# A fused attention and mixture-of-experts kernel: a regrouped start, spread side operations, and TensorE taking value matmuls before score matmuls in each step

## The chip, the cores and the metric

The kernel runs on one core of one Trainium2 chip. The metric is device microseconds (us) of one execution. The core has five engines with queues of their own: TensorE (PE, matmuls; PEld is its weight load), VectorE (DVE), ScalarE (ACT), GpSimd (POOL) and SyncE (SP), which here only issues DMAs. Engines run in parallel and meet at semaphores; each engine takes its own instructions in program order, so an instruction that waits holds up all that stand behind it.

## The reference

The input is x, 2048 rows of 128 (f32). Three sublayers follow each other:

```python
# causal attention, 16 heads of width 8, with rotary positions
Q = rope((x @ wq.T) by heads); K = rope((x @ wk.T) by heads); V = (x @ wv.T) by heads
scores = where(causal, Q K^T / sqrt(8), -inf)
x = layernorm(x + (softmax(scores) @ V) @ wo.T)
# inner block: attention without a mask, then 8 experts with top-1 routing
y = x + softmax(Q2 K2^T / sqrt(8)) V2 @ w_proj      # Q2, K2, V2 from layernorm(x) @ w_qkv
y = y + expert[argmax(h @ gate_w + gate_b)](h)       # h = layernorm(y); 128 -> 512 -> gelu -> 128
x = layernorm(x + y)
```

So there are two attentions over 2048 positions: number 1 is causal, number 2 is full.

## The kernel before

**Tiling.** The 2048 queries are cut into 4 blocks (`NB`) of 512 (`BLK`), and the keys into tiles of 128. The 16 heads go in 4 groups (`G`) of 4. One *step* is one key tile, one query block and one group: 4 heads x 128 keys x 512 queries. A step has two halves p = 0 and 1 of two heads each. In block qb a group has T steps: 16 in attention 2, 4(qb+1) in attention 1, where the tiles past the diagonal are left out. So attention 1 has 160 steps and attention 2 has 256. The last four steps of each causal group lie on the diagonal: there the query range shrinks (512, 384, 256, 128 queries), and POOL clears the upper triangle (`cut`, line 925, `affine_select` in line 930).

**One half-step.** `scores` (571): two matmuls of 33 rows (32 rows hold the parts of the heads' q and k, row 33 the negative row shift against a row of ones) into a pair of PSUM banks; three pairs rotate, so the scores of half h wait for the exponentials of half h-3. `exps` (823): one ACT instruction reads 128x1024 scores and writes probabilities. It waits for the scores of its half and for the values of half h-4. `values` (581): four columns of the array take 9 columns of V each and add into PSUM bank 6; they wait for the exponentials of the same half, and on the diagonal for POOL's clearing of it. At a group's end DVE copies bank 6 out (`evac`, 1187), PE transposes it (`turn`, 605, three steps into the next group) and DVE divides by the sums (`norm`, 1192).

**The order in a step** is written out in PE's `group` (690 to 719). In step kt PE first issues both halves of the scores of step kt, then the second half of the values of step kt-2 and the first half of those of step kt-1. After that come the turn and the *side operations* of this step: a table `side` says at which step of the block which one stands. DVE follows the same step numbers through `due(step)`.

**Side operations.** In attention 1 (`side1`, 769), while block qb runs, the block before is finished: `post_turn` (5), `post_project` (7), `z_turn` (14), both projections of keys and queries in one call (`project2`, 16), the values (18), key and query norms (20), and `lows` in steps 21 to 24. `lows` samples scores for a lower bound of each row's maximum: in each of these steps two bf16 matmuls into the one PSUM bank 7, each reduced by DVE (`tensor_reduce`, line 1273) before the next may write. Block 3 has no later block to hide behind: its side work stands between the attentions, its `lows` on four banks. In attention 2 the side work is routing and experts.

**Row shifts.** `settle` (534 and 1137) turns norms into the shift of block 0's rows; `final` and `shift_row` (328), or `first_shift_row` (846) on ACT's DMA queue for block 0, write it into `query_rows`. The shifts of blocks 1 to 3 are worked out in block 0's shadow. `general` is a slow exact fallback behind a flag; here the flag is not set, and it costs a flag read and a copy to `negf`. It also times the shift row of the next block: in the last group of a block.

**The start.** For each block PE projects (`project1`), DVE rotates (`split1`, 1054), POOL adds and splits k (`split_k`, 914) between clearing memory with memsets (984), ACT rounds and squares (`first_parts`, 853). SP sends the parts to DRAM (`to_scratch`, 303) and reads them back in row layout (`key_rows`, 308, four DMAs; `query_rows`, 316, eight). SP takes the blocks in order: parts 0, key rows 0, query rows 0, parts 1, key rows 1, parts 2, key rows 2, parts 3, key rows 3, query rows 1, and then two DMAs that fill two rows of `key_rows` with ones (355). Each read-back waits until its parts have landed. Attention 1 waits for the ones (`ld_pad`), block 0's rows, its shift row and all four value projections.

Of the kernel before, what the change touches and what calls it, by code (L numbers as in the profile page):

```python
# [21 lines left out]
ALU = mybir.AluOpType  # L22
# [10 lines left out]
H = 16  # L33
# [37 lines left out]
SHIFT_AT = (None, 4, 6, 8, 9)  # L71
# [18 lines left out]
OPS = len(IN_SHADE)  # L90

# [5 lines left out]
def build(nc, xT_d, x_d, wa_d, wo_d, wqkv_d, wproj_d, ln1w_d, ln1b_d, ln2w_d, ln2b_d, gw_d, gb_d,  # L97
          w1_d, w2_d, cos_d, sin_d, ident_d, blk_d, cmask_d, iota_d, kc_d, out_d):
    ctx = ExitStack()
    with ctx:  # L100
# [121 lines left out]
        ld_a, ld_w, ld_x, ld_e, ld_pad = (sem(n) for n in ("ld_a", "ld_w", "ld_x", "ld_e", "ld_pad"))  # L222
        ld_b = [sem(f"ld_b{b}") for b in range(NB)]
        ld_m, ld_k, z_clear = sem("ld_m"), sem("ld_k"), sem("z_clear")
        init, ones_set, rows_clear = sem("init"), sem("ones_set"), sem("rows_clear")
# [31 lines left out]

        def low_bank(b, i, c):

            return ps[:, 7 if b < NB - 1 else (2 * i + c) % 4, :]  # L260
# [23 lines left out]
        def _(sp):  # L284
# [56 lines left out]
            for b in range(NB):  # L341
# [3 lines left out]
                to_scratch(1, k3, k_scratch, b)  # L345
                sp.wait_ge(A[1]["parts_out"][b % 2], 32 * (b // 2 + 1))
# [3 lines left out]
                if b == 0:  # L350
                    query_rows(1, b)
# [30 lines left out]
            slot_free(2, 1)  # L382
            query_rows(2, 1)
# [36 lines left out]
        def _(pe):  # L420
# [30 lines left out]
            def project2(b):  # L451
# [3 lines left out]
                mm(ps7, wqkv[:, D:2 * D], hT[:, :]).then_inc(s["k_proj"], 1)  # L455
                if b < NB - 1:
                    pe.wait_ge(s["k_taken"], b + 1)
# [25 lines left out]
            def key_bound(a):  # L483

                s = A[a]
                pe.wait_ge(s["kdiag"], 1)
                mm(ps[:, 7, 0:H], onesf[0:H, :], kdg[:, :]).then_inc(s["kmb_mm"], 1)
# [15 lines left out]
            def lows(b, i):  # L503

                t = b * TB + i
                if t == 0:
                    pe.wait_ge(kbd, 1)
                pe.wait_ge(A[2]["nq_taken"], b + 1)
                turn_taken(1)
                for c in range(H * NSUB // BLK):  # L510
                    n = 2 * t + c
                    pe.wait_ge(low_taken, n if b < NB - 1 else max(2 * (NB - 1) * TB, n - 3))
# [982 lines left out]
```

## Time and profile before

| | us |
|---|---|
| median of 3 runs (lowest, highest) | 1136.85 (1129.67, 1142.27) |
| the profiled execution | 1127.68 |
| its span | 1125.9 |
| PE busy | 900.4 (80%) |
| ACT busy | 782.9 (70%) |
| DVE busy | 362.0 (32%) |
| POOL busy | 239.9 (21%) |

The span is what the profiler saw from the first to the last instruction; 1.8 us lie around it. Busy times of PE count matmuls that overlap in the array as one. The granted TensorE clock of the whole span is 0.888 of full speed.

### The profile page before, as it was taken

How to read it: one execution, taken by the hardware profiler on the slowest of the kernel's cores; microseconds unless marked ns; L12 is line 12 of the kernel's file. 1: busy time of each engine (PE TensorE's matmuls, PEld its weight loads, DVE VectorE, ACT ScalarE, POOL GpSimd, SP SyncE). 2: the span in 40 equal slices, each digit the busy share in tenths (PEclk: the TensorE clock that was granted, in tenths of full speed). 3: DMA queues.
4: the chain of work that ended last, by engine and by line, in shares of the span. 5: the costliest groups of instructions: out<-in, count | busy, mean ns of one | idle time of the engine just before them, and what ended most of it. 6: DMA issues, size and time to landing. Idle time of an engine off the chain costs nothing.

```text
span 1125.9 us, 24400 instructions
## 1 busy us (share of the span) xinstructions
PE 900.4 (80%) x9813; PEld 400.4 (36%) x9820; DVE 362.0 (32%) x1027; ACT 782.9 (70%) x906; POOL 239.9 (21%) x360
## 2 busy tenths in 40 slices
PE   5401898897998799439999999999999999996262
PEld 2200443343444334214333444444344444443131
DVE  4440225244014200550000323324433254333563
ACT  1201675785996789119999998898988989884140
POOL 6700411111111101100000032321433212332233
PEclk9655979898998989659999999999999999997565
DMA  7685021111000711273000200012100000000101
GB/s 240 111 160 60 3 40 38 19 23 39 2 2 1 111 22 30 47 161 89 1 2 2 39 25 2 2 28 37 34 2 3 25 11 25 2 2 25 33 1 33
DMA packets 30546, 43.17 MB, mean 38 GB/s; under 512 B 3936, under 2 KB 14944, under 8 KB 30432
## 3 DMA queue, kind: packets, MB, share of 16 engines
q1 hardware_dynamic: 28832, 37.85, 16.8%
q0 software_dynamic: 1536, 3.67, 1.1%
q8 instruction: 79, 1.29, 0.5%
q14 instruction: 35, 0.29, 0.1%
q10 hardware_dynamic: 64, 0.07, 0.0%
HBM read 28.73 MB, written 12.45 MB: 37 GB/s over the span
## 4 chain that ended last, share of the span: by engine, by line
PE 66%; DVE 11%; DMA 9%; ACT 5%; issue 4%; SPq 2%; POOL 1%; another core or an unknown queue 1%; POOLq 0%; ACTq 0%; DVEq 0%
PE ps L422 61%; DMA k_scratch<-parts 4%; ACT probs L829 4%; PE ps L427 3%; DMA key_rows<-ones_f 2%; DVE row_low L1273 1%; PE ps L675 1%; DMA y_sorted<-early_late 1%; DMA query_rows<-neg_shift_final 1%; SPq L322 1%; ACT squares_blockdiag L843 1%; DMA z_rows<-y_sorted,row_shift 1%; POOL z_rows L970 1%; SPq L314 1%
## 5 line engine op out<-in xcount | busy, mean ns | idle before, releaser
L829 ACT ACTIVATE probs<-ps 128x1024 f32<-128x1024 f32 (+3 forms) x832 | 742.8, 1011 | 195.2 <-PE ps L422 193.1
L422 PE MATMUL ps<-probs,values 128*9 128x256 f32 (+1 forms) x6528 | 436.9, 381 | 6.5 <-DVE q_rotated L1190 6.2
L422 PE MATMUL ps<-query_rows,key_rows 33*128 33x512 f32 (+3 forms) x1664 | 337.0, 465 | 73.1 <-DMA key_rows<-ones_f 42.6
L422 PEld LDWEIGHTS ps<-query_rows,key_rows 33*128 33x128 f32 x1664 | 143.0, 190 | 266.8 <-ACT probs L829 119.1
L422 PEld LDWEIGHTS ps<-probs,values 128*9 128x9 f32 x6528 | 145.1, 91 | 220.1 <-issue 120.8
L930 POOL TENSOR_SCALAR_AFFINE_SELECT probs<-probs 128x256 f32<-128x256 f32 x128 | 52.3, 409 | 344.4 <-ACT probs L829 342.0
L1190 DVE COPY q_rotated<-ps 128x512 f32<-128x512 f32 x32 | 22.1, 690 | 217.5 <-PE ps L422 217.4
L963 POOL COPY expert_stage<-early_late 128x512 f32 x72 | 45.4, 668 | 162.1 <-PE ps L422 162.1
L944 POOL DMA_INDIRECT z_sorted<-z_rows,row_shift x16 | 15.8, 990 | 237.3 <-issue 177.0
L959 POOL COPY expert_stage<-parts 128x512 f32 x72 | 47.9, 707 | 44.6 <-PE ps L422 39.1
L900 ACT ACTIVATE expert_stage<-parts 128x512 f32 x24 | 15.1, 630 | 48.7 <-DVE row_shift L1322 27.6
L1197 DVE RECIPROCAL recip<-ps 128x16 f32<-128x16 f32 x32 | 8.2, 257 | 98.0 <-PE ps L427 98.0
L1354 DVE COPY k_work<-ps 128x512 f32<-128x512 f32 x24 | 16.6, 690 | 62.9 <-PE ps L675 62.9
L422 PE MATMUL ps<-expert_stage,k_work 128*32 128x128 f32 x576 | 29.3, 301 | 4.1 <-issue 2.4
L1273 DVE TENSOR_REDUCE row_low<-ps 128x8 f32<-128x512 f32 x32 | 22.1, 692 | 22.2 <-PE ps L422 13.5
L422 PEld LDWEIGHTS ps<-expert_stage,k_work 128*32 128x32 f32 x576 | 24.2, 122 | 13.6 <-issue 6.2
L422 PE MATMUL ps<-early_late,w_attn 128*128 128x512 f32 x32 | 19.9, 780 | 11.4 <-DMA early_late<-in_sin 7.3
L422 PE MATMUL ps<-early_late,k_work 128*32 128x128 f32 x192 | 29.0, 301 | 0.0
L984 POOL MEMSET key_rows<- 32x4096 f32 x8 | 28.0, 3504 | 0.9 <-POOL row_ok L974 0.5
L1129 DVE TENSOR_SCALAR neg_shift<-ps 16x512 bf16<-16x512 f32 x8 | 5.4, 676 | 68.1 <-PE ps L427 68.1
L427 PE MATMUL ps<-ident,z_rows 128*128 128x128 f32 x32 | 6.2, 326 | 22.5 <-DVE z_rows L1051 12.6
L422 PE MATMUL ps<-expert_stage,h_cols 128*32 128x512 f32 x128 | 20.2, 709 | 4.4 <-ACT expert_stage L900 3.3
(166 smaller groups left out, 612.9 us busy)
## 6 DMA issues: line engine op xcount, KB each, us to landing
query_rows<-q_scratch SPq DMA_DIRECT2D x64, 128.0 KB
key_rows<-k_scratch SPq DMA_DIRECT2D x20, 256.0 KB, 7.2
q_scratch<-parts SPq DMA_DIRECT2D x8, 512.0 KB, 3.7
k_scratch<-parts SPq DMA_DIRECT2D x8, 512.0 KB, 4.0
key_rows<-k_scratch SPq DMA_DIRECT2D x16, 192.0 KB, 6.4
parts<-in_w SPq DMA_DIRECT2D x1, 2048.0 KB, 8.3
early_late<-in_w SPq DMA_DIRECT2D x8, 256.0 KB, 7.3
early_late<-z_sorted SPq DMA_DIRECT2D x4, 384.0 KB, 3.1
```

Source lines behind the costliest of these rows:

```text
L422: return nc.tensor.matmul(out, l, r, start=start, stop=stop, skip_group_check=True)
L427: last = nc.tensor.transpose(out[0:m, i * P:(i + 1) * P], rows(i), ident[:, :])
L829: nc.scalar.activation(Pr[:, i % 2, 2 * p:2 * p + 2, lo:BLK], score_banks(t, p)[:, :, lo:BLK], ACT.Exp, scale=SCALE).then_inc(s["exp"], 1)
L900: nc.scalar.activation(w1s[g], W1[:, bass.ds(e * HID, HID)], ACT.Copy).then_inc(m_w1, 1)
L930: nc.gpsimd.affine_select(out=at, in_=at, compare_op=ALU.is_ge, fill=0.0, base=0, pattern=[[0, 2], [1, P]], channel_multiplier=-1).then_in ...
L944: nc.gpsimd.indirect_dma_start(out=z_sorted, out_offset=bass.IndirectOffsetOnAxis(ap=dest[:, i:i + 1], axis=0), in_=zb[:, i, :], in_offset ...
L959: nc.gpsimd.tensor_copy(w1s[g], W1[:, bass.ds(e * HID, HID)]).then_inc(m_w1, 1)
L963: nc.gpsimd.tensor_copy(w2s[g], W2[:, bass.ds(e * HID, HID)]).then_inc(m_w2, 1)
L984: link(nc.gpsimd.memset(KA[at:at + ROWS, part].bitcast(F32), 0.0))
L1190: copy(accs[:, :], sums).then_inc(s["evac"], 1)
L1273: mark(nc.vector.tensor_reduce(low[:, t, hs], low_bank(b, i, c).rearrange("p (h t) -> p h t", t=NSUB), AX.X, ALU.max), low_taken, 2 * t + ...
L1354: mark(copy(hTs2[:, :], side), m_taken, n)
```

## The change

- **Start.** Block 0 is settled alone (norms, bound, shift, flag) after two projections; blocks 1 to 3 follow. The sum and the split of q move from DVE to POOL (`split1` on POOL, `rotate1` and `norms1` on DVE). The memsets between blocks and the ones DMAs go; all 32 pad rows become 1.0, by two ACT copies, one DVE memset and one POOL memset of 32x8192 elements each at the very start. SP's order becomes: parts 0, key rows 0, query rows 0, parts 1, shift row 0, parts 2, key rows 1, query rows 1, parts 3, key rows 2, key rows 3. The key bound is spread a second time for blocks 1 to 3 (`key_bound(1, 2)` at step 0).
- **Side operations.** `project2` is cut in two, each of the eight `lows` matmuls of a block gets a step of its own, and the steps stand in a table `SIDE1_AT` for each block.
- **Block 3's `lows`** move from between the attentions into steps 4 to 11 of attention 2's block 0; its shift turns move to steps 17 to 25. `query_rows(2, 1)` is issued after the first shift row has landed.
- **`general`** of the causal block 0 runs one group earlier.
- **Order in a step.** PE takes the values first and the scores second.

```diff
-SHIFT_AT = (None, 4, 6, 8, 9)
+SHIFT_AT = {1: (None, 5, 6, 8, 9), 2: (None, 17, 21, 23, 25)}
+LOWS_AT = tuple(range(4, 12))
+SIDE1_AT = {
+    1: (13, 14, 15, 17, 20, 21, (22, 23, 24, 25, 26, 28, 29, 30)),
+    2: (13, 17, 19, 21, 23, 25, (28, 30, 32, 34, 36, 38, 40, 42)),
+    3: (14, 17, 20, 22, 24, 26, (28, 30, 32, 34, 36, 38, 40, 42)),
+}
...
+def general_group(causal, qb):
+    return G - 2 if causal and qb == 0 else G - 1
...
+            parts_sent(0)
+            first_key_rows(0)
+            query_rows(1, 0)
+            parts_sent(1)
+            shift_row(1, 0)
+            parts_sent(2)
+            first_key_rows(1)
             query_rows(1, 1)
-            sp.wait_ge(rows_clear, 1)
-            for at in (ROWS, HALF + ROWS):
-                sp.dma_start(kaf[at:at + 1, :, :].rearrange("o h (c t) -> o (h c) t", t=P),
-                             onesf[0:1, :].unsqueeze(1).to_broadcast([1, PAIRS * S // P, P])).then_inc(ld_pad, 16)
+            parts_sent(3)
+            first_key_rows(2)
+            first_key_rows(3)
...
-            slot_free(2, 1)
-            query_rows(2, 1)
             sp.wait_ge(A[2]["parts_out"][1], 64)
...
-            sp.wait_ge(low_mm, 2 * S // P)
             sp.wait_ge(A[2]["c_row"], 32)
+            slot_free(2, 1)
+            query_rows(2, 1)
...
                 for kt in range(T):
-                    for p in range(2):
-                        scores(s, qb % 2, g, kt * P, t0 + kt, mine[kt]["lo"], p)
                     if kt == 0 and before is not None:
                         values(a, before[-2], 1)
                         values(a, before[-1], 0)
...
                     if kt >= 2:
                         values(a, mine[kt - 2], 1)
                         values(a, mine[kt - 1], 0)
+                    for p in range(2):
+                        scores(s, qb % 2, g, kt * P, t0 + kt, mine[kt]["lo"], p)
...
+            project1(0)
+            project1(1)
+            key_norms(1, 0)
+            query_norms(1, 0)
             settle(1)
+            general(1, 0, 0)
+            for b in range(1, NB):
+                if b + 1 < NB:
+                    project1(b + 1)
+                key_norms(1, b)
+                query_norms(1, b)
             attention(1, side1, after1)
...
-            for i in range(TB):
-                lows(b, i)
             settle(2)
...
+            act.wait_ge(ones_set, 1)
+            for at in (ROWS, HALF + ROWS):
+                nc.scalar.activation(KAv[at:at + ROWS, :, S // 2:S],
+                                     onesf[at:at + ROWS, 0:1].unsqueeze(2).to_broadcast([ROWS, PAIRS, S // 2]),
+                                     ACT.Copy).then_inc(rows_set, 1)
...
+            link(nc.gpsimd.memset(KAv[ROWS:2 * ROWS, :, 0:S // 2].bitcast(F32), 1.0))
...
+            nc.vector.memset(KAv[HALF + ROWS:P, :, 0:S // 2].bitcast(F32), 1.0).then_inc(rows_set, 1)
...
+            rotate1(0)
+            norms1(0)
+            rotate1(1)
             settle(1)
+            general(1, 0)
```

## Rows read from the trace of the kernel before

**Rows 1.** The page's chain of waits: shares of the span by engine.
```profile
PE 66%; DVE 11%; DMA 9%; ACT 5%; issue 4%; SPq 2%; POOL 1%; another core or an unknown queue 1%; POOLq 0%; ACTq 0%; DVEq 0%
```

**Rows 2.** Windows by stage: length, busy PE, PEld, DVE, ACT, POOL, clock, DMA, GB/s.
```profile
0.00:107.60 107.60, 30.03 (x110) 14.96 (x110) 37.27 (x88) 11.96 (x21) 40.47 (x22) 0.67 0.74 149
107.60:142.40 34.80, 28.27 (x302) 14.17 (x302) 6.41 (x17) 20.90 (x32) 13.00 (x32) 0.84 0.02 5
142.40:456.80 314.40, 282.62 (x2972) 122.38 (x2976) 86.69 (x253) 242.97 (x288) 39.31 (x96) 0.93 0.18 31
456.80:499.80 43.00, 12.08 (x44) 6.59 (x46) 29.35 (x101) 2.56 (x5) 3.10 (x2) 0.62 0.39 75
499.80:1026.30 526.50, 511.89 (x6084) 221.71 (x6088) 151.55 (x415) 486.13 (x530) 112.36 (x169) 0.99 0.09 22
```

**Rows 3.** Chain of waits in the start: start us, us, what.
```profile
33.80 19.58 DMA k_scratch<-parts
...
88.54 19.01 DMA key_rows<-ones_f
```

**Rows 4.** Timeline of the start: start us, us, engine, line, operation, [idle before <-releaser].
```profile
3.47 7.07 POOL L984 MEMSET key_rows<- 32x4096 f32 x2 [0.47 <-POOL row_ok L974]
...
53.45 0.63 ACT L861 ACTIVATE parts<-k_work 128x512 fp32r<-128x512 f32 x1 [10.95 <-DMA k_scratch<-parts]
```

**Rows 5.** Timeline at the first scores of attention 1's block 1.
```profile
141.59 1.22 PE L422 MATMUL ps<-query_rows,key_rows 33*128 33x512 f32 x4 [4.86 <-DMA query_rows<-neg_shift_final]
```

**Rows 6.** Timeline of PE in one step of attention 2 without side work.
```profile
603.65 0.91 PE L422 MATMUL ps<-query_rows,key_rows 33*128 33x512 f32 x4
...
604.49 1.05 PE L422 MATMUL ps<-probs,values 128*9 128x256 f32 x16
605.47 0.19 PEld L422 LDWEIGHTS ps<-query_rows,key_rows 33*128 33x128 f32 x2 [0.43 <-issue]
```

**Rows 7.** Timeline of ACT over the same stretch.
```profile
602.95 11.14 ACT L829 ACTIVATE probs<-ps 128x1024 f32<-128x1024 f32 x12
```

**Rows 8.** Timeline where ACT waits for scores, and PE then for ACT.
```profile
129.91 0.73 PE L422 MATMUL ps<-query_rows,key_rows 33*128 33x512 f32 x4
...
130.50 1.02 ACT L829 ACTIVATE probs<-ps 128x1024 f32<-128x1024 f32 x1 [0.90 <-PE ps L422]
...
500.71 2.86 ACT L829 ACTIVATE probs<-ps 128x1024 f32<-128x1024 f32 x3 [24.24 <-PE ps L422]
501.78 0.29 PEld L422 LDWEIGHTS ps<-query_rows,key_rows 33*128 33x128 f32 x2 [1.04 <-ACT probs L829]
```

**Rows 9.** Timeline of one diagonal step: exponentials, then POOL's clearing.
```profile
123.73 3.35 ACT L829 ACTIVATE probs<-ps 128x1024 f32<-128x1024 f32 x4 [0.91 <-PE ps L422]
...
125.00 0.41 POOL L930 TENSOR_SCALAR_AFFINE_SELECT probs<-probs 128x256 f32<-128x256 f32 x1 [1.62 <-ACT probs L829]
```

**Rows 10.** Groups by form: exponentials over 256 queries; busy, mean ns.
```profile
L829 ACT ACTIVATE probs<-ps 128x512 f32<-128x512 f32 x32 | 18.9, 641 | 5.8 <-PE ps L422 5.7
```

**Rows 11.** Windows: a causal group, a full group, a full group with experts.
```profile
298.10:318.80 20.70, 20.18 (x238) 8.71 (x236) 1.72 (x5) 19.84 (x24) 3.19 (x9) 1.00 0.01 3
...
561.60:591.30 29.70, 29.35 (x328) 11.68 (x326) 1.30 (x4) 29.44 (x33) 0.00 (x0) 1.00 0.01 2
684.80:720.40 35.60, 34.87 (x462) 15.67 (x464) 12.32 (x22) 31.52 (x37) 13.69 (x23) 1.00 0.01 2
```

**Rows 12.** Timeline of PE: scores of two neighbouring steps that hold sampled scores.
```profile
373.37 0.73 PE L422 MATMUL ps<-query_rows,key_rows 33*128 33x512 f32 x4
...
376.58 0.73 PE L422 MATMUL ps<-query_rows,key_rows 33*128 33x512 f32 x4
```

**Rows 13.** Timeline between the attentions.
```profile
477.07 5.77 DVE L1273 TENSOR_REDUCE row_low<-ps 128x8 f32<-128x512 f32 x8 [0.55 <-remote]
...
490.71 1.32 ACTq L851 DMA_DIRECT2D query_rows<-neg_shift_final  x2
...
499.82 1.65 PE L422 MATMUL ps<-query_rows,key_rows 33*128 33x512 f32 x6 [10.67 <-DMA query_rows<-neg_shift_final]
```

More of the change, by code:

```diff
@@ L339, in slot_free, with parts_sent @@
                     sp.wait_ge(A[1]["S"], 2 * first_step(True, NB - 1 + b))
-            for b in range(NB):
+            def parts_sent(b):
                 sp.wait_ge(A[1]["q_split"], b + 1)
@@ L501, in query_norms, with lows @@
                 last.then_inc(s["nq_mm"], 1)
-            def lows(b, i):
-                t = b * TB + i
-                if t == 0:
+            def lows(b, n):
+                i, c = n // 2, n % 2
+                if b == n == 0:
                     pe.wait_ge(kbd, 1)
                 pe.wait_ge(A[2]["nq_taken"], b + 1)
[L509 to L512, printed above, removed]
-                    mm(low_bank(b, i, c), sq[:, 2, i * P:(i + 1) * P], kblk[:, c * BLK:(c + 1) * BLK]).then_inc(low_mm, 1)
+                turn_taken(1 if b < NB - 1 else 2)
+                if b == NB - 1:
+                    pe.wait_ge(A[2]["flag"], 1)
+                pe.wait_ge(low_taken, 2 * b * TB + n)
+                mm(ps7, sq[:, 2, i * P:(i + 1) * P], kblk[:, c * BLK:(c + 1) * BLK]).then_inc(low_mm, 1)
             def shift_turn(a, b):
@@ L712, in group @@
                         values(a, mine[kt - 1], 0)
+                    for p in range(2):
+                        scores(s, qb % 2, g, kt * P, t0 + kt, mine[kt]["lo"], p)
                     if kt == TURN_STEP and n:
                         turn(a, n - 1, after.get(g))
[L715 removed]
+                        if g == general_group(causal, qb) and qb + 1 < NB:
                             general(a, qb + 1, t0 + TURN_STEP + 1)
@@ L726, in attention @@
                     pe.wait_ge(s["q_taken"], NB)
-                general(a, 0, 0)
+                if not causal:
+                    general(2, 0, 0)
                 mine = None
@@ L763, in side0 @@
             def side0(a):
-                todo = {SHIFT_AT[b]: [lambda b=b: shift_turn(a, b)] for b in range(1, NB)}
-                todo[SHIFT_AT[NB]] = [lambda: count_ok(a, 2)]
+                at = SHIFT_AT[a]
+                todo = {at[b]: [lambda b=b: shift_turn(a, b)] for b in range(1, NB)}
+                todo[at[NB]] = [lambda: count_ok(a, 2)]
+                if a == 1:
+                    todo[0] = [lambda: key_bound(1, 2)]
+                else:
+                    for n, p in enumerate(LOWS_AT):
+                        todo[p] = [lambda n=n: lows(NB - 1, n)]
                 return todo
@@ L806, in _ @@
             query_norms(2, b)
-            for i in range(TB):
-                lows(b, i)
             settle(2)
@@ L1237, in split2 @@
                 if b < NB - 1:
+                    due(at[2])
                     dve.wait_ge(s["q_proj"], b + 1)
@@ L1252, in split2 @@
                     mark(tt(sq[:, 0, :], qa[:, :], qa[:, :], ALU.mult), s["sq_q"], b + 1)
-                    due(18)
+                    due(at[3])
                     dve.wait_ge(s["v_proj"], b + 1)
@@ L1369, in attention @@
                 causal = a == 1
-                general(a, 0)
                 if causal:
@@ L1373, in attention @@
                 else:
+                    general(2, 0)
                     link(ts(before[:, :], cmask[:, :], 0.0, None, ALU.is_lt))
@@ L1383, in attention @@
                     if qb + 1 < NB:
-                        events.append(((G - 1) * T + TURN_STEP, lambda: general(a, qb + 1)))
+                        events.append((general_group(causal, qb) * T + TURN_STEP, lambda: general(a, qb + 1)))
                     events.sort(key=lambda e: e[0])
@@ L1408, in attention @@
                     else:
+                        if causal:
+                            spread_key_norms(1, 2)
+                        else:
+                            take_lows(NB - 1, LOWS_AT, due)
                         shift(a, 1, NB)
                         for b in range(1, NB):
-                            due(SHIFT_AT[b])
+                            due(SHIFT_AT[a][b])
                             take_shift(a, b)
-                        due(SHIFT_AT[NB])
+                        due(SHIFT_AT[a][NB])
                         take_ok(a, 2)
```

126 lines of the change are left out of this document (63 added, 63 removed).

## The prediction

> **What bounds it now.** I read the chain of waits first: 66% of the span hangs on PE, 5% on ACT [rows 1]. Such a share mixes stages, so the windows by stage come next [rows 2]. Five stretches matter. In the start, 107.6 us, PE is busy for 30 and the DMA engines for 0.74 of the time; the chain there is two long transfers, 19.6 us for the parts of block 1 and 19.0 us until the ones have landed [rows 3]. Block 0 of attention 1 takes 34.8 us, its blocks 1 to 3 take 314.4, the gap between the attentions 43.0, attention 2 takes 526.5. After that a tail follows that the change does not touch.
>
> What bounds a step is read from the timeline, and it decides this case. A step of attention 2 without side work takes 1.82 us on PE: 0.84 for both score halves, 0.98 for both value halves [rows 6]. ACT does 12 exponentials in 11.14 us without a break [rows 7]; less the last one's own 1.02, that is 0.92 per half, 1.84 per step. So both run at one pace, and ACT is never without work, because PE issues the scores of step kt before it waits for the exponentials that its values need.
>
> **The order in a step.** Before: S(2k), S(2k+1), V(2k-3), V(2k-2), where S, V and E of a number are scores, values and exponentials of that half. After: V(2k-3), V(2k-2), S(2k), S(2k+1). V(2k-2) waits for E(2k-2), and now S(2k) stands behind it in PE's queue, and E(2k) waits for S(2k). That closes a loop from E(2k-2) to E(2k), once per step. Its pieces:
> - an exponential that found no backlog took 1.02 us [rows 8];
> - PE went on 0.05 after its end: start 500.71 plus 1.02 is 501.73, the weight load began at 501.78 [rows 8];
> - a value half is half of 0.98, 0.49 [rows 6]; I take 0.55, as the change of operands to the scores lies behind this half alone;
> - from the first score matmul to the start of the exponential 0.59 (129.91 to 130.50) [rows 8].
>
> Sum 2.2 us per step against 1.83: plus 0.37. The bounds are 2.1 (value half 0.49, start of the exponential 0.05 sooner) and 2.3 (if the exponentials stay as long as with backlog for part of the steps). One step of each group escapes: at kt=1 only one value half stands ahead, whose exponential is old, so it stays at 1.83. In a step with side work X, PE has 2.2 minus its own 1.82 to spare before V(2k) is due, so a step costs the larger of 2.2 and what it cost before; it is not the sum.
>
> *Attention 2.* A group without side work took 29.7 [rows 11]; it becomes 15 x 2.2 + 1.83 = 34.8, plus 5.1. Block 0 has four such: plus 20. The `lows` and shift turns put there are a few tenths of PE each, in steps of their own, and fit in the spare 0.38. In blocks 1 to 3 a group with experts took 35.6 [rows 11], 2.2 on average, but mixed from steps of 1.83 and longer ones. By the step tables 25 of a block's 64 steps carry side work; the other 39 go up by 0.37: 14, less about 1 for the four steps after a group's end, where the wait for the copy of the sums is now inside the loop. Three blocks: 39. Together plus 59, less 2 for the same wait in block 0: **plus 57**. With 2.1 or 2.3 in place of 2.2 it is 42 or 73.
>
> *Attention 1, blocks 1 to 3.* Full-width steps behave alike. On the diagonal V(2k-2) waits for POOL too. The first exponential there ended at 123.73 + 1.02 = 124.75, POOL began at 125.00 and took 0.41 [rows 9]; PE's reaction I put at 0.1 (between nothing and POOL's own 0.25). That is 0.76 in place of 0.05, in the loop. Before, the two score halves and V(2k-3) covered it. The exponentials shrink from 1.02 to 0.64 at half width [rows 10], so by 0.19 per tile; value and score parts shrink from 1.14 in all to an estimated 0.7. The four diagonal steps become about 2.9, 2.6, 2.2, 1.7 = 9.4. A quiet group of 12 steps took 20.7 [rows 11]: 8 x 1.83 = 14.6 and 6.1 for the diagonal. It becomes 8 x 2.2 + 9.4 - 0.4 = 26.6. Groups of 8 and 16 steps go from 13.4 to 17.8 and from 28.0 to 35.4. Four groups of each: from 248 to 319.
>
> *Side operations.* The stretch really took 314.4 [rows 2], so 66 lie above its quiet groups: side work, waits and stretches at the lower clock. A step with two sampled scores took 3.21 (373.37 to 376.58) [rows 12], 1.39 more than a quiet one, twelve times: 17. Each now has a step, one matmul, and a reduction of 0.7 on DVE that has the whole step: nothing. Of the other 49, the projections and z turns mostly sink into the spare 0.38 of more steps. I leave 30: two post steps per block, the excess of four large side matmul groups, waits for DVE's chains, and half-clock stretches after the diagonals, where PE will be busy for less than half of 9 us. If nothing of the 49 sinks it is 49, if the low clock stays away 18. 319 + 30 = 349 against 314: **plus 35** (23 to 54).
>
> **The start.** The memsets: POOL cleared 32x8192 elements in 7.07 [rows 4], and POOL and DVE pay that once while the inputs load. ACT's copy of 512 elements took 0.63 [rows 4], so at most 10 us for 8192, with 1.02 for 1024 as the nearer price 8; two end at 16 to 22, when ACT's first rounding is due at about 17: no loss to 5 us. Sum and split of q move to POOL, 1.27 each there, two more per block; POOL has lost 28 us of memsets. Block 0's parts go out about 1 us later. Then SP's queue decides: parts 1 stand behind key rows 0 and query rows 0 as before, landed at 53.4 [rows 3, 4]. Block 3's rounding on ACT waits for them, and v_taken of block 3 gates attention 1. Shift row 0 stands right behind parts 1 and its flag comes at about 35, so it lands by 56. Attention 1 starts at **58** rather than 107.6, 49 sooner.
>
> But block 1 of attention 1 can't follow as soon. SP still has parts 2, key rows 1, query rows 1, parts 3, key rows 2 and 3 to move, and only then shift row 1. That is what filled 53.4 to 107.6 before, less the ones, some 4 us: about 105 with the shift row's own 2. Block 0's 16 steps are all diagonal: 4 x 9.4 = 38, and at the lower clock, in which the start ended (0.67 over the stretch [rows 2]), 2 more per group and 4 for the turns: 50, ending at 108. Both give the first scores of block 1 at **about 107**, against 141.6 with its 4.9 us wait for the shift row [rows 5]: **minus 35**. Bounds: 100 (full clock) and 115 (ACT's copies late, low clock throughout). `general` a group sooner removes that 4.9, which is in this number; what is late next is that same shift row, behind key rows 3.
>
> **The gap.** Eight reductions, 5.8 us, stood alone on DVE [rows 13]. The shift row was issued at 490.7 to 492.0 and scores began at 499.8: 7.8 for two 16 KB transfers, behind the eight query-row transfers of block 1 that SP had just issued. These now follow it; I take 2 to 3 us for it. Minus 5.8 and minus 5: **minus 11** (6 to 12). Query rows 1, W1 and W2 are needed a block later.
>
> **Sum**: 57 + 35 - 35 - 11 = plus 46, on the profiled execution's 1127.7: 1174. That execution lies 9.2 below the median of 1136.85 and below all three runs, so I forecast 1174 + 9 = **1183** as a median.
>
> **Rivals.**
> *The loop is covered (faster).* Should the exponential of S(2k) start without waiting for V(2k-2) to pass, nothing is lost in the order: minus 35, minus 36 (66 to 30 in the side work), minus 11 give 1046, 1055 as a median. It decides at a loop of 1.83, which needs 0.37 of the 1.19 us of latency and matmuls to vanish. For it speaks that matmul ends are modelled; against it that PE issues in program order and each piece has a row. 0.08.
> *Half covered.* The loop is nearer 2.0, the diagonals cost half, and the side work sinks wholly: 1125 to 1150. 0.13.
> *The clock.* PE gets gaps of 0.38 us in each step of attention 2, where the granted clock was 0.99 with PE busy for 512 of 526.5 [rows 2]. At 1.2 GHz PE's own work is 2 x 1.82 = 3.64 per step, so attention 2 would take 930 and the whole about 1500; a fifth of the steps, 1250. Against it: block 0 of attention 1 held 0.84 with PE busy for 28 of 34.8 [rows 2], less than the 83% to come. 0.04. The Trainium skill (TensorE: Matmul & The Clock Gate, "A second HAM failure mode: psum-queue depth-cycling") has a matmul kernel whose frequent micro-idles made the clock swing between its two levels; by that rule this rival would be the likely one, and the rows of attention 2 can't refute it, since they hold no such gaps.
> *The start is not earlier.* If ACT's copies or POOL's longer chain delay parts 1 by 10 us, both ends of the start move: 1193 to 1215. 0.08.
>
> The likeliest has the remaining 0.67, 1150 to 1210. I count 1% (11 us of the median) as no change. Slower: 0.67, 0.12 from clock and start, 0.02 of the half-covered: 0.81. Within: 0.08. Faster: 0.08 and 0.03: 0.11. The range of 8 in 10 reaches from 1128 to 1212.
>
> **What would show it.** ACT's exponentials at 1.02 us each, with a gap before every other one, released by PE scores; starts of score pairs 2.2 apart; a quiet full group of 34.8 and a quiet causal group of 12 steps of 26.6; weight loads of the values waiting for ACT and, on the diagonal, POOL; first scores at 58, block 1's at 107, and a gap of 32. Quiet full groups at 29.7 would make the forecast wrong; so would attention 2 at a clock well under 1.

## The result, and the profile after

The change made the kernel slower: 1179.88 us as the median of 4 runs (1171.62 to 1189.43) against 1137.38 for the kernel before on the same chip (1129.67 to 1142.27, 4 runs), a ratio of 1.0356 with a 95% interval of 1.0264 to 1.0448. Forecast were 1183, in a range of 1128 to 1212. Ratios leave out slow executions, more than 1.5% above the fastest of their kernel, which the medians keep, so that a ratio here can differ a little from the quotient of two medians. The profiled execution has a span of 1184.6 us, 58.7 above that of before.

The windows by stage come first, as before, cut at PE's first scores of each stage (columns as in [rows 2]):

```profile
0.00:55.40 55.40, 26.97 (x110) 13.91 (x110) 34.02 (x60) 26.36 (x23) 30.52 (x23) 0.85 0.80 202
55.40:96.50 41.10, 32.70 (x314) 13.95 (x312) 14.20 (x41) 20.47 (x32) 12.99 (x32) 0.79 0.84 125
96.50:449.90 353.40, 304.69 (x2927) 111.18 (x2939) 83.84 (x248) 246.93 (x286) 38.14 (x94) 0.86 0.13 25
449.90:491.20 41.30, 15.04 (x73) 8.97 (x65) 22.04 (x80) 3.21 (x7) 4.08 (x5) 0.57 0.39 71
491.20:1083.50 592.30, 527.23 (x6037) 192.82 (x6040) 160.19 (x440) 500.40 (x528) 112.85 (x169) 0.99 0.10 21
```

Compare PE's share in the last line: 527 of 592, where it was 512 of 526.5 [rows 2]. PE has a little more to show as busy and 50 us more in which it waits. The stages of all kernels below are cut at the first and the last exponential of each stage, which gives slightly other lengths than [rows 2]:

| us | before | after | difference | forecast |
|---|---|---|---|---|
| start | 108.5 | 56.3 | -52.2 | |
| attention 1, block 0 | 34.0 | 41.2 | +7.2 | -35 with the start |
| attention 1, blocks 1 to 3 | 309.2 | 353.4 | +44.2 | +35 |
| gap | 49.1 | 41.3 | -7.7 | -11 |
| attention 2 | 524.0 | 592.4 | +68.4 | +57 |
| tail | 101.2 | 100.0 | -1.2 | 0 |
| span | 1125.9 | 1184.6 | +58.7 | +46 |

**The loop.** The chain of waits by engine, first line of that part of the page, has changed its owner in part: ACT had 5% of the chain [rows 1] and now has 22.

```profile
PE 55%; ACT 22%; DVE 6%; issue 6%; DMA 6%; POOL 2%; SPq 2%; POOLq 1%; ACTq 1%; DVEq 0%
```

The timeline shows the whole loop in a quiet step of attention 2 (start us, us, engine, line, operation, count, [idle before <-releaser]):

```profile
605.92 1.94 ACT L862 ACTIVATE probs<-ps 128x1024 f32<-128x1024 f32 x2 [0.29 <-PE ps L437]
605.98 0.12 PEld L437 LDWEIGHTS ps<-probs,values 128*9 128x9 f32 x8 [0.37 <-ACT probs L862]
605.98 0.62 PE L437 MATMUL ps<-probs,values 128*9 128x256 f32 x8
607.00 0.12 PEld L437 LDWEIGHTS ps<-probs,values 128*9 128x9 f32 x8 [0.90 <-ACT probs L862]
607.00 0.62 PE L437 MATMUL ps<-probs,values 128*9 128x256 f32 x8 [0.39 <-ACT probs L862]
607.54 0.30 PEld L437 LDWEIGHTS ps<-query_rows,key_rows 33*128 33x128 f32 x4 [0.43 <-issue]
607.55 0.73 PE L437 MATMUL ps<-query_rows,key_rows 33*128 33x512 f32 x4
608.14 1.94 ACT L862 ACTIVATE probs<-ps 128x1024 f32<-128x1024 f32 x2 [0.29 <-PE ps L437]
```

Follow it once round. The first of the pair of exponentials starts at 605.92 and takes 1.02, so it ends at 606.94. PE starts its values at 607.00, 0.06 later. The scores start at 607.55, 0.55 after that. ACT starts on them at 608.14, 0.59 later. 1.02 + 0.06 + 0.55 + 0.59 = 2.22, and 608.14 - 605.92 = 2.22. Every piece stands where the forecast had it. ACT rests 0.29 in each step and PE 0.39; neither engine is full, and each waits for the other.

Windows of whole groups: a quiet full group of attention 2, a causal group of 12 steps in attention 1, and 4 us just after a diagonal:

```profile
566.60:601.90 35.30, 29.88 (x326) 9.18 (x324) 1.30 (x4) 30.94 (x33) 0.00 (x0) 1.00 0.01 2
...
172.60:203.00 30.40, 26.89 (x250) 9.97 (x248) 10.82 (x48) 20.60 (x24) 3.26 (x8) 0.78 0.24 33
...
205.00:209.00 4.00, 4.00 (x32) 1.75 (x32) 0.81 (x1) 1.82 (x2) 0.00 (x0) 0.50 0.01 4
```

The first answers to the 29.70 of [rows 11]. A quiet causal group of 12 steps, forecast at 26.6, doesn't occur: the four groups of block 2 took 30.0 to 34.8. In the second the clock is 0.78, in the third 0.50, which is the lower of its two levels, 1.2 GHz, and PE is busy all the time: the wait on the diagonal is followed by slow matmuls.

**The diagonal** has POOL's clearing in the same loop (timeline, last full-width step of a group):

```profile
367.55 1.94 ACT L862 ACTIVATE probs<-ps 128x1024 f32<-128x1024 f32 x2 [0.29 <-PE ps L437]
...
368.73 0.41 POOL L972 TENSOR_SCALAR_AFFINE_SELECT probs<-probs 128x256 f32<-128x256 f32 x1 [29.73 <-ACT probs L862]
...
369.29 0.62 PE L437 MATMUL ps<-probs,values 128*9 128x256 f32 x8 [0.74 <-POOL probs L972]
...
369.84 0.62 PE L437 MATMUL ps<-query_rows,key_rows 33*128 33x384 f32 x4
370.38 1.51 ACT L862 ACTIVATE probs<-ps 128x768 f32<-128x768 f32 x2 [0.90 <-PE ps L437]
```

367.55 to 370.38 is 2.83 for this step. The three after it take 2.57, 2.08 and 2.03 where nothing else disturbs them, 9.5 in all. In block 2, where the clock is often at the lower level, the four took 10.9 to 13.1.

**The start.** The chain of waits in the start (start us, us, what), and then PE's first scores of block 0 and of block 1:

```profile
33.31 17.36 DMA k_scratch<-parts
...
59.29 22.71 DMA k_scratch<-parts
...
83.88 10.49 DMA key_rows<-k_scratch
```

```profile
55.38 1.22 PE L437 MATMUL ps<-query_rows,key_rows 33*128 33x512 f32 x4
...
96.54 1.22 PE L437 MATMUL ps<-query_rows,key_rows 33*128 33x512 f32 x4
```

**The gap**, timeline of its last part:

```profile
476.71 1.26 POOL L1035 TENSOR_TENSOR parts<-q_work,parts 128x512 f32<-128x512 f32 x1 [24.85 <-ACT q_work L922]
477.09 0.89 DVE L1121 TENSOR_TENSOR k_norm_max<-k_norm_max 16x1 f32<-16x1 f32 x1
...
477.91 1.89 POOL L1038 COPY values<-early_late 128x2048 f32<-128x2048 f32 x1
...
478.27 1.55 DVE L1126 TENSOR_SCALAR k_norm_diag<-ident,k_norm_max 16x16 f32<-16x16 f32 x1
...
487.65 1.90 ACTq L884 DMA_DIRECT2D query_rows<-neg_shift_final  x2
...
491.24 0.80 PE L437 MATMUL ps<-query_rows,key_rows 33*128 33x512 f32 x2 [5.15 <-DMA query_rows<-neg_shift_final]
```

The shift row went out at 487.65, 3.1 earlier than before [rows 13], and scores followed 3.6 later where it had been 9.1. The two DVE operations at 477.09 and 478.27 are odd: on 16 partitions, and 0.89 and 1.55 us long. More on them at the end.

### The profile page after: what moved, and what is told of

It is laid out like the page before. It is cut to its first block, busy times and chain, and to the rows that moved or that the text cites. A ratio compares the mean times of both kernels' runs of the same rounds, so it can differ in the third digit from the quotient of the medians.

```text
span 1184.6 us, 24409 instructions
## 1 busy us (share of the span) xinstructions
PE 943.3 (80%) x9808; PEld 361.8 (31%) x9822; DVE 365.2 (31%) x1022; ACT 817.6 (69%) x908; POOL 230.5 (19%) x361
## 4 chain that ended last, share of the span: by engine, by line
PE 55%; ACT 22%; DVE 6%; issue 6%; DMA 6%; POOL 2%; SPq 2%; POOLq 1%; ACTq 1%; DVEq 0%
PE ps L437 51%; ACT probs L862 20%; DMA k_scratch<-parts 4%; PE ps L442 2%; PE ps L694 1%; ACT key_rows L899 1%; POOL probs L972 1%; DMA key_rows<-k_scratch 1%; SPq L329 1%; SPq L321 1%; POOL z_rows L1012 0%; DMA z_rows<-y_sorted,row_shift 0%; DMA y_sorted<-early_late 0%; DVE ln_stats L1079 0%; DVE squares_blockdiag L1371 0%
## 5 line engine op out<-in xcount | busy, mean ns | idle before, releaser
L862 ACT ACTIVATE probs<-ps 128x1024 f32<-128x1024 f32 (+3 forms) x832 | 763.1, 973 | 235.7 <-PE ps L437 235.5
L437 PE MATMUL ps<-probs,values 128*9 128x256 f32 (+1 forms) x6528 | 501.2, 391 | 118.3 <-ACT probs L862 81.9
L437 PE MATMUL ps<-query_rows,key_rows 33*128 33x512 f32 (+3 forms) x1664 | 318.5, 460 | 6.4 <-DMA query_rows<-neg_shift_final 5.2
L437 PEld LDWEIGHTS ps<-probs,values 128*9 128x9 f32 x6528 | 118.3, 91 | 421.0 <-ACT probs L862 327.4
L437 PEld LDWEIGHTS ps<-query_rows,key_rows 33*128 33x128 f32 x1664 | 135.0, 197 | 192.2 <-issue 158.4
L437 PE MATMUL ps<-expert_stage,k_work 128*32 128x128 f32 x576 | 29.2, 300 | 4.3 <-DVE attn_rows L1237 1.6
L442 PE MATMUL ps<-ident,q_rotated 128*128 128x128 f32 x128 | 21.9, 296 | 1.7 <-DVE q_rotated L1227 1.7
L437 PEld LDWEIGHTS ps<-early_late,k_work 128*32 128x32 f32 x192 | 21.3, 120 | 0.0
```

The lines of the kernel that those rows point to most:

```text
L437: return nc.tensor.matmul(out, l, r, start=start, stop=stop, skip_group_check=True)
L442: last = nc.tensor.transpose(out[0:m, i * P:(i + 1) * P], rows(i), ident[:, :])
L862: nc.scalar.activation(Pr[:, i % 2, 2 * p:2 * p + 2, lo:BLK], score_banks(t, p)[:, :, lo:BLK], ACT.Exp, scale=SCALE).then_inc(s["exp"], 1)
```

## The experiments

All ratios are to the kernel before, with 95% intervals. First the order in a step alone, in both directions; then the parts of the rest.

**1. The change without its new order.** The changed kernel, with the scores first in each step as before.

```diff
                 for kt in range(T):
+                    for p in range(2):
+                        scores(s, qb % 2, g, kt * P, t0 + kt, mine[kt]["lo"], p)
...
                         values(a, mine[kt - 1], 0)
-                    for p in range(2):
-                        scores(s, qb % 2, g, kt * P, t0 + kt, mine[kt]["lo"], p)
```

> The changed kernel with the order in a step put back: both score halves first, then the value halves. If the loop E(2k-2), V(2k-2), S(2k), E(2k) is what the new order costs, a quiet step of attention 2 goes from 2.23 back to 1.83 us, attention 2 from 592 to about 524 to 530 between its first and last exponential, blocks 1 to 3 of attention 1 from 353 to about 280, and the span is about 97 + 280 + 41 + 526 + 100 = 1044. If the steps are long for another reason (the side operations in more steps, or the lower clock), the quiet step stays above 2.0 and the span above 1120.

Measured: 1058.56 us (1054.49 to 1062.89), ratio 0.9246 (0.9172 to 0.9321). So all the rest of the change is worth 7.5%, and the order costs more than all of it. Windows of blocks 1 to 3 of attention 1 and of attention 2:

```profile
96.60:373.80 277.20, 267.34 (x2937) 115.92 (x2939) 84.86 (x248) 241.33 (x286) 38.70 (x93) 0.96 0.17 32
...
412.60:951.20 538.60, 516.35 (x6025) 221.28 (x6025) 158.45 (x440) 486.81 (x528) 112.66 (x169) 0.98 0.11 23
```

353.4 against 277.2 and 592.3 against 538.6: with the start and the gap at about the same length, the order costs 76 and 54 us in these two stages. The clock in the first went from 0.96 to 0.86 with it. Attention 2 lies 9 us above the 530 expected here; the last section follows them up to a hold-up of PE.

**2. The new order alone.** The kernel before with the same few lines moved the other way: values first, nothing else of the change.

```diff
                 for kt in range(T):
-                    for p in range(2):
-                        scores(s, qb % 2, g, kt * P, t0 + kt, mine[kt]["lo"], p)
...
+                    for p in range(2):
+                        scores(s, qb % 2, g, kt * P, t0 + kt, mine[kt]["lo"], p)
```

> The kernel before with only the order in a step changed: values first, scores second. By the loop: quiet steps of 2.23 in place of 1.82, attention 2 about 590 rather than 524, blocks 1 to 3 of attention 1 about 365 rather than 309, block 0 about 42 rather than 34, the start unchanged at 108: a span of about 1250. If the order does its harm only together with the spread side operations, the span stays under 1180.

Measured: 1286.50 us (1283.00 to 1293.88), ratio 1.1221 (1.1138 to 1.1305). A quiet full group in its windows is the same 35.30 as in the changed kernel:

```profile
658.80:694.10 35.30, 29.87 (x326) 9.12 (x324) 1.31 (x4) 30.90 (x32) 0.00 (x0) 1.00 0.01 2
```

The span of 1292 is 42 above the expected 1250: blocks 1 to 3 took 382 where 365 stood, with the clock at 1.2 GHz for 121 us of them, and attention 2 took 604 where 590 stood.

The four kernels make a square. The order multiplies the time by 1.122 on the old rest and by 1.0356 / 0.9246 = 1.120 on the new one; within the intervals these are equal. In microseconds they are less alike, 143 and 121 by the medians. One reason is visible: block 0 takes 9.7 longer with the order on the old rest and no longer on the new one, where in either order it ends with a wait for block 1's shift row.

**3. Scores between the value halves.** The loop says that only V(2k-2), whose exponential is fresh, must not stand ahead of the scores. Here PE takes V(2k-3), S(2k), S(2k+1), V(2k-2) (at kt=2 both value halves behind the scores).

```diff
+                    elif kt >= 3:
+                        values(a, mine[kt - 2], 1)
+                    for p in range(2):
+                        scores(s, qb % 2, g, kt * P, t0 + kt, mine[kt]["lo"], p)
...
-                        values(a, mine[kt - 2], 1)
                         values(a, mine[kt - 1], 0)
-                    for p in range(2):
-                        scores(s, qb % 2, g, kt * P, t0 + kt, mine[kt]["lo"], p)
```

> The changed kernel with a third order: the old value half V(2k-3), then both score halves, then V(2k-2). Only the value half whose exponential is old stands ahead of the scores, so the loop is open. By the loop theory the quiet step is 1.83 and the span within 10 us of that of the scores-first order, 1035 to 1055. If it is putting values ahead of scores as such that costs (switching of operands twice a step, later scores), the quiet step is 1.95 or more and the span 1080 or more.

Measured: 1086.08 us (1084.50 to 1091.45), ratio 0.9477 (0.9408 to 0.9546). The quiet step is 1.81, as with the scores first: it is that one value half which closes the loop, not the place of values as such. But the kernel is 27.5 us slower than the first experiment, where at most 10 were expected. A quiet group takes 30.1 in place of 29.6, and the timeline shows the step with the transposes, two halves of values and a turn between two pairs of scores:

```profile
506.50 0.73 PE L437 MATMUL ps<-query_rows,key_rows 33*128 33x512 f32 x4
...
507.71 0.66 PE L442 MATMUL ps<-ident,q_rotated 128*128 128x128 f32 x4
...
508.85 0.73 PE L437 MATMUL ps<-query_rows,key_rows 33*128 33x512 f32 x4
509.45 2.86 ACT L865 ACTIVATE probs<-ps 128x1024 f32<-128x1024 f32 x3 [0.34 <-PE ps L437]
```

From scores to scores 2.35, and ACT ran dry for 0.34 before it. This step is 2.29 long by its exponentials, and 1.85 with the scores first. So in this step the score pairs come too late behind the old value half and the transposes. That accounts for some 0.45 us in each group of attention 2; the rest of the 27.5 was not traced step by step (blocks 1 to 3 are 19 us longer, with 40 us at 1.2 GHz against 20, and attention 2 is 11 longer).

**4 and 5. No clearing on the diagonal**, in the changed kernel (values first) and in the first experiment (scores first). Both leave out the masking on the diagonal: POOL does nothing there, and the values wait for the exponentials alone.

```diff
-                             cut=2 * (n * TB + kt % TB) + 1 if causal and kt >= qb * TB else None,
+                             cut=None,
...
-                    if causal:
-                        with pool.Fori(0, G) as g:
-                            group(qb, g)
```

> The changed kernel (values first) without POOL's clearing of the upper triangle on the diagonal and without PE's wait for it; the masking is left out, nothing else. If POOL's 0.25 + 0.41 + 0.1 us stand in the loop on the diagonal, the last four steps of a causal group shorten from 9.5 to about 6.7 to 7 us, 64 steps by 0.7 each: a span some 40 to 50 us shorter, 1135 to 1145, a little less still if the clock is lower for less of the time. If the clearing is hidden, as it was before, the span stays at 1175 to 1185.

Measured: 1146.12 us (1140.30 to 1149.49, 10 runs), ratio 1.0000 (0.9964 to 1.0036).

> The changed kernel with scores first and without POOL's clearing of the upper triangle and PE's wait for it; the masking is left out. A control for the run without clearing and values first. If the clearing is covered by the scores and by V(2k-3) in this order, the time stays within 10 us of the scores-first run (1055 of span). If the clearing costs by itself, wherever it stands, the span is some 30 to 40 us shorter here too.

Measured: 1038.58 us (1036.69 to 1047.66), ratio 0.9223 (0.9143 to 0.9304). Windows with values first: two causal groups of 12 steps; then with scores first: blocks 1 to 3 whole.

```profile
219.20:243.50 24.30, 22.22 (x246) 7.58 (x244) 4.29 (x9) 20.59 (x24) 0.00 (x0) 1.00 0.07 26
243.50:267.90 24.40, 22.04 (x242) 7.50 (x240) 4.48 (x9) 20.62 (x25) 0.00 (x0) 1.00 0.01 3
```

```profile
98.50:369.10 270.60, 261.68 (x2946) 115.41 (x2957) 82.82 (x248) 241.59 (x287) 0.00 (x0) 0.98 0.17 32
```

In blocks 1 to 3 the clearing costs 353.4 - 305.7 = 48 us behind the values and 277.2 - 270.6 = 7 us behind the scores. Without it the last four steps of a group take 2.17, 1.90, 1.41 and 1.36, 6.85 in place of 9.5; over 12 groups that is 32. The other 16 I put down to the clock: it was at 1.2 GHz for 95 us of these blocks in the changed kernel and for 10 without the clearing. The blocks fit this on the whole: 4 x 2.65 is 10.6, and with the clearing block 1, with 7 of the 95 us, is 7.6 longer, block 3, with 20, is 10.2 longer, and block 2, with 68, is 29.9 longer. (In the same stage the kernel before had 44, the first experiment 20.)

The kernel with scores first became 19.9 shorter by its span, more than the 10 of a covered clearing and less than the 30 of one that isn't. 7 are the clearing's; 12.6 lie in attention 2, which has nothing to clear (see the last section).

**6. The old side table on the first experiment.** Scores first, all else of the change, but the side operations in the old steps, `lows` two per step.

```diff
-SIDE1_AT = {
-    1: (13, 14, 15, 17, 20, 21, (22, 23, 24, 25, 26, 28, 29, 30)),
...
-}
+SIDE1_AT = {q: (14, 16, 16, 18, 20, 20, (21, 21, 22, 22, 23, 23, 24, 24)) for q in (1, 2, 3)}
...
-                    todo[p] = [lambda n=n: lows(b, n)]
+                    todo.setdefault(p, []).append(lambda n=n: lows(b, n))
```

> The changed kernel with scores first and with the side operations of attention 1 at the step numbers of the kernel before (two sampled scores a step again, keys and queries in one step). If spreading them is worth what the steps of 3.2 us showed, blocks 1 to 3 of attention 1 go from 277 up to about 305, near the 309 of the kernel before, and the span to about 1083. If it is not the spreading but the earlier start or the clock that made that stretch shorter, it stays at 277 to 285.

Measured: 1073.85 us (1071.08 to 1077.59), ratio 0.9518 (0.9445 to 0.9592). Blocks 1 to 3 take this in the windows, with a clock of 0.95 in place of 0.96:

```profile
98.40:401.60 303.20, 274.19 (x2947) 119.21 (x2951) 84.68 (x248) 242.19 (x287) 38.50 (x95) 0.95 0.15 29
```

303.2 against 277.2: spreading is worth 26 us there. The spans differ by 15.5 only: the rest is lost in attention 2, where the two kernels are the same code and yet the first experiment takes 538.7 and this one 528.0; see the last section. The medians lie 15 apart as well, the ratios 0.027, which is 31 us: the two were timed on different chips, and the executions of the kernel before that are in the ratio have a median of 1129.2 here and of 1143.9 there. The size in the whole is between 15 and 31.

**7. The shift row of block 1 before the key rows.** In the first experiment PE finished block 0 at about 85 and then waited; the chain of waits there shows for what:

```profile
84.75 0.69 SPq L339
...
85.48 10.90 DMA query_rows<-neg_shift_final
```

DVE had started on the last copy of the row at 79.3, but SP issued it behind the key rows of blocks 2 and 3, and its two small transfers took 10.9 us among theirs. This edit moves it up:

```diff
             parts_sent(3)
+            shift_row(1, 1)
             first_key_rows(2)
             first_key_rows(3)
```

> The changed kernel with scores first and with shift row 1 issued before key rows 2 and 3. In the profile with scores first, block 0 was done at 85, the shift row was issued at 84.7 and landed at 96.4 behind key rows 3. If that queue place is what block 1 waits for, its first exponential comes at 86 to 88 rather than 97.5 and the span goes from 1055 to about 1045. If block 1's own key and query rows are late as well, it stays at 95 or more.

Measured: 1036.79 us (1031.80 to 1054.41, 7 runs), ratio 0.9170 (0.9112 to 0.9228). It was run again beside a repeat of the first experiment:

> The changed kernel with scores first, once more, beside the next one on the same chip: a span of 1035 to 1058, the spread coming from short stretches at the lower clock in attention 2.

> Scores first and shift row 1 ahead of key rows 2 and 3, once more, beside the run before on the same chip: 10 to 13 us less than it, all of it before the first scores of block 1.

Measured: the first experiment again 1056.62 us (1050.80 to 1058.99), ratio 0.9237 (0.9163 to 0.9312); the early shift row again 1048.88 (1045.70 to 1057.34), ratio 0.9166 (0.9101 to 0.9232). The timelines of SP and PE of this last one:

```profile
81.78 1.35 SPq L339 DMA_DIRECT2D query_rows<-neg_shift_final  x2
83.25 5.11 SPq L321 DMA_DIRECT2D key_rows<-k_scratch  x8
```

```profile
86.83 0.73 PE L439 MATMUL ps<-query_rows,key_rows 33*128 33x512 f32 x4
```

Block 1 starts at 86.8 in place of about 97, and block 0 takes 29.2 where it took 40.1: 11 us, as the chain had promised. By medians 7.8 of them arrive, and the two intervals overlap. In the profiled execution attention 2 was 6 longer, with 38 us at 1.2 GHz against 17 in the repeat of the first experiment. So the gain at its place is shown, its size in the whole is not. By its ratio it is the fastest version of all, 8.3% under the kernel before.

**8. The ones without their DMAs, on the kernel before.** POOL's memsets write 1.0 in place of 0.0, and the two DMAs at the end of SP's start go.

```diff
-            for at in (ROWS, HALF + ROWS):
-                sp.dma_start(kaf[at:at + 1, :, :].rearrange("o h (c t) -> o (h c) t", t=P),
-                             onesf[0:1, :].unsqueeze(1).to_broadcast([1, PAIRS * S // P, P])).then_inc(ld_pad, 16)
...
-                    pe.wait_ge(ld_pad, 32)
+                    pe.wait_ge(rows_clear, 1)
...
-                    link(nc.gpsimd.memset(KA[at:at + ROWS, part].bitcast(F32), 0.0))
+                    link(nc.gpsimd.memset(KA[at:at + ROWS, part].bitcast(F32), 1.0))
```

> The kernel before with the two ones DMAs taken away: POOL's memsets between the blocks write 1.0 rather than 0.0, and attention 1 waits for them in place of the DMAs. The prediction put the ones at some 4 us of the DMA stretch and so block 1's first scores in the changed kernel at 107; they came at 97. If the ones cost about 4, attention 1 starts at 103 to 105 here rather than 107.6. If they were the mis-sized piece, it starts at 96 to 99 and the span is about 10 us shorter. If it starts at 104 or later, what was faster in the changed kernel is the order of its transfers.

Measured: 1116.81 us (1110.92 to 1121.59), ratio 0.9781 (0.9709 to 0.9854). The end of the start in its chain of waits, and the issue of block 0's shift row in its timeline:

```profile
67.32 7.91 DMA key_rows<-k_scratch
75.23 0.11 issue
75.34 1.55 PE ps L419 x6
```

```profile
65.51 1.91 ACTq L848 DMA_DIRECT2D query_rows<-neg_shift_final  x2
```

First scores at 75.3 against 107.6: 32 us from these two transfers alone, where at most 12 were expected. The chain names key rows, but PE needs only those of block 0 here, and they had landed at 35.6; the wait that ended last is the one for block 0's shift row, whose last piece landed at 75.20. In the kernel before it had landed at 76.14, so attention 1 then waited 31 us for the ones alone. Those 31 us are not the ones' own time. Just ahead of them in SP's queue stand block 1's query rows. From their issue to the last landing it took 25.3 us with the ones (82.29 to 107.55) and 22.9 without (81.02 to 103.95). So the ones made the run of transfers only some 2.3 us longer, and cost 32 because they stood at its end. By medians 27.7 arrive; in the profiled execution it is 16.8, as 13.7 are given back in attention 2.

## Why the prediction was right, and where it was off

The direction and the mechanism were right: the order closes a loop from exponential to exponential, and what the rest of the change gains is less than what that costs. Point by point:

**The loop of 2.2 us.** Measured 2.23 per quiet step, from pieces of 1.02, 0.06, 0.55 and 0.59 against 1.02, 0.05, 0.55 and 0.59. The step at kt=1 stayed at 1.83 as said. A quiet full group took 35.3 where 34.8 stood.

**Attention 2, +57, measured +68.4.** (The upper bound, worked out with 2.3, comes to 76 and not 73.) In blocks 1 to 3 it is 44 where 39 stood: the quiet step is 0.42 longer, not 0.37, and 39 steps of three blocks make 6 of that. Block 0 went up by 24.7 where 18 stood. Its first group took 39.2 in place of 31.3: the clock was at 1.2 GHz for the first 14.2 us of attention 2, against 7 before, and there the steps took 3.0 to 3.55. The forecast had no term for that.

**Blocks 1 to 3 of attention 1, +35, measured +44.2.** The diagonal was right at full clock: 9.4 said, 9.5 measured. The mis-sized term is the low clock behind it, priced at about 12 us. It was there for 95 us in place of 44, and the fourth experiment puts 16 us of time on the clock that the clearing brings. The side operations behaved as the first experiment shows: with the scores first, these blocks fell from 309.2 to 277.2, by 32, where the fall from 66 to 30 in this term had said 36. So the two halves of the term were +76 for the order (said: 71) and -32 for the rest (said: -36).

**Start and block 0, -35, measured -45.** First scores at 55.4 where 58 stood; block 1's at 96.5 where 107 stood, outside the bounds of 100 and 115 on the good side. The step that failed is "That is what filled 53.4 to 107.6 before, less the ones": it takes the same transfers to need the same time in a new order. The ones were not what was mis-sized: 4 said, 2.3 by the eighth experiment. But from the landing of parts 1 to the last row of this stretch there were 51.9 us there (52.02 to 103.95) and 43.7 in the changed kernel (50.67 to 94.37), so 8 us went with the order. In the old order block 1's eight query-row transfers stand last; from 92 to 104 us they keep the DMA engines busy for 0.46 of the time in the eighth experiment. In the new order they are issued at 53.3, land at 79.3 and share that time with parts 2 and 3, at a share of 0.86 to 1.11 from 55 to 75 us. No run changed that order alone, so the 8 us are a difference of two traces. The key rows of block 3 landed at 94.4 where 103 stood. That block 0 would take 50 us was wrong too: its steps took 36, near the 38 said for full clock, and with 4 us of waiting for block 1's shift row it came to 41. The two errors had the same sign. The wait for block 1's shift row behind the key rows, named as the next thing late, was real: the seventh experiment takes it away and gains 11 us at that place with the scores first.

**The gap, -11, measured -7.7.** The transfers gave 5.5 where 5 stood. The 5.8 us of reductions gave only 2.2. Behind them stood DVE's own chain of norms and now two of its operations waited for POOL instead.

**The sum.** +58.7 by the profiled executions against +46. That the forecast of 1183 lies 3 from the median of 1180 is partly luck: the profiled execution after (1184.6 of span) was above its median, the one before was below. The terms were off by 10, 9, 3 and 11 us, with one of them on the other side. By the medians the difference is 42.5, so the two ways to measure it lie 16 us apart, more than any of these errors.

**The rivals.** The loop covered was refuted by the trace, and its figure of 1055 is near what the same kernel does with the scores first, 1058.56. That is partly luck: by parts the first experiment shows -45, -32, -10 and, in attention 2, +15, where that sum had -35, -36, -11 and nothing. The loop half covered fell with the 2.23. The start not earlier fell with first scores at 55.4. The clock: from 506.4 to the end of attention 2 this window shows 1.00 (the columns are those of [rows 2]), with PE resting 0.39 in each quiet step.

```profile
506.40:1083.50 577.10, 512.86 (x5945) 187.96 (x5945) 159.50 (x439) 490.81 (x518) 112.85 (x169) 1.00 0.08 19
```

The pattern told in the Trainium skill (TensorE: Matmul & The Clock Gate, "A second HAM failure mode: psum-queue depth-cycling") did not come here in attention 2. What did come is that waits on the diagonals are followed by stretches at 1.2 GHz, 95 us of blocks 1 to 3 against 10 without the clearing.

## What to carry to other kernels

In a queue that is worked in order, put the work that feeds the next engine ahead of the work that waits for that engine's last result; a single half ahead of it turned a step of 1.81 us into one of 2.23, though neither engine was full. Find the price before building by adding the pieces of the loop from rows where that engine had no backlog. And when a transfer or an operation goes, read what the waiting engine needs otherwise: the price of the ones was the distance to the next wait, block 0's shift row 32 us earlier, though they had made the run of transfers only 2.3 us longer.

## What the runs showed of the hardware

**DVE behind POOL.** In the gap an operation on 16x1 elements took 0.89 us and one on 16x16 took 1.55. They ended at 477.98 and 479.82; POOL's add ended at 477.97 and its copy at 479.80. The second of these took 0.22 in the kernel before, where the eight reductions held DVE until POOL was done. The Trainium skill (SBUF — State Buffer, "Summary: rules for kernel authors") says that the one issued second waits until the first is done if DVE works in its mode with two ports, or has two inputs in SBUF while the GpSimd operation reads SBUF. The ends in this trace agree; which of the two the 16x16 operation meets, the trace doesn't tell. In the first experiment POOL's add began 0.10 after the first of these two and not 0.38 before it: the two took 0.15 and 0.66, and the second again ended 0.02 after POOL's add. No run here moved the copy away, so how much of the gap it would give was not measured.

**A hold-up of PE that the profile does not explain.** The first group of experts in attention 2 is the same code in all kernels, but for the order in a step. Here are its windows in the first experiment and in the scores-first kernel without clearing, and the rows behind the difference, from the timeline of the first in block 2:

```profile
568.60:603.30 34.70, 31.79 (x342) 12.79 (x334) 6.56 (x11) 30.70 (x34) 10.65 (x16) 0.95 0.07 21
```

```profile
561.00:592.10 31.10, 30.33 (x342) 12.44 (x334) 6.54 (x11) 30.21 (x34) 10.66 (x16) 1.00 0.07 22
```

```profile
710.40 0.50 PE L437 MATMUL ps<-query_rows,key_rows 33*128 33x512 f32 x2 [0.23 <-issue]
712.35 1.02 ACT L862 ACTIVATE probs<-ps 128x1024 f32<-128x1024 f32 x1 [2.00 <-PE ps L437]
713.43 0.50 PE L437 MATMUL ps<-query_rows,key_rows 33*128 33x512 f32 x2 [2.53 <-ACT probs L862]
```

PE's wait ends with the exponential that is named, at 713.37. It is this exponential that is late: it starts 1.95 after its scores, where 0.59 was the delay in the loop above, and ACT waits for PE until then. So PE's matmuls at 710.40 were reported done some 1.4 late, and what held them no row shows. Such a hold-up, and a stretch of 3.4 us at 1.2 GHz behind it, come at the start of this group in all three blocks, 3.6 to 4.3 us each, in the first experiment, its repeat and the eighth. By the lengths of these groups they come, smaller or larger, in the second, third and seventh too, and in the changed kernel without clearing; not in the kernel before, the changed one, the sixth, or the scores-first kernel without clearing. They account for 11 of the 12.6 us by which attention 2 is shorter there than in the first experiment, though it has nothing to clear, and for the 11 by which it is shorter with the old side table. The eighth experiment differs from the kernel before by two DMAs in the start and has it. Which property of the program decides stays open. Until it is known, a difference of 10 us between two builds of this kernel can't be put down to their edits without looking at this group.
